# One program for both rounds of local attention and feed-forward, with the next stage's first products among a stage's last steps

## The reference

```python
def _layer(x, wqkv, qs, ksc, wo, lg, lb, w1, b1, w2, b2):
    h = shift_token(x)                      # half the features from the token before
    q, k, v = jnp.split(h @ wqkv, 3, axis=-1)          # 8 heads of 64
    q, k = rotary_xpos(l2norm(q) * qs, l2norm(k) * ksc)
    o = local_attention(q, k, v)            # windows of 64, own and preceding window
    x = x + o @ wo
    h = layernorm(shift_token(x)) * lg + lb
    a, g = jnp.split(h @ w1 + b1, 2, axis=-1)          # 341 features each
    return x + (a * gelu(g)) @ w2 + b2
for l in range(2):
    x = _layer(x, wqkv[l], ...)
```

## Time and profile before

| | |
|---|---|
| three runs | 1767.3, 1768.34, 1778.39 us; median 1768.34 us |
| the profiled execution | span 1763.0 us from its first to its last instruction; the median is 5.3 us more, and no other time of this execution is given |
| busy share of the span | TensorE 90%, VectorE 79%, ScalarE 67%, GpSimd 45% |
| second block | from 778.0 us (first L1319) to 1506.6 us (last instruction ahead of the barrier) |
| its stages begin at | 778.0 (attention), 1063.7 (feed-forward), 1138.8 (attention), 1423.4 (feed-forward) |

### The profile page before, as it was taken

How to read it: one execution, slowest core, us unless ns; L and a number is a source line. 1 busy time by engine, 2 the same in 40 slices (tenths; PEclk the granted TensorE clock), 3 DMA queues, 4 the chain that set the end, 5 groups by cost and what they waited for, 6 DMA issues and landing times. The chain is left out here.

```text
span 1763.0 us, 41286 instructions
## 1 busy us (share of the span) xinstructions
PE 1593.1 (90%) x14986; PEld 813.6 (46%) x14986; DVE 1391.9 (79%) x2949; ACT 1187.9 (67%) x2461; POOL 787.4 (45%) x607
## 2 busy tenths in 40 slices
PE   7499999999999999959999988889999989799887
PEld 4122323322323322236777765557777645444454
DVE  6799999999999999358999976479999869343355
ACT  5178888888888888847787872267878734455521
POOL 4211111221111224338888862188888825544301
PEclk9589999999999999979999999989999999799999
DMA  5203110000000100112232222212232222000001
GB/s 166 70 19 127 43 43 20 20 20 20 21 23 23 30 20 2 49 54 52 61 72 68 57 49 74 54 42 60 55 99 56 56 51 63 1 1 1 1 14 36
DMA packets 124306, 79.02 MB, mean 45 GB/s; under 512 B 50579, under 2 KB 110925, under 8 KB 123853
## 3 DMA queue, kind: packets, MB, share of 16 engines
q1 hardware_dynamic: 122716, 75.31, 16.2%
q10 hardware_dynamic: 1392, 1.12, 0.2%
HBM read 42.82 MB, written 16.79 MB: 34 GB/s over the span
## 5 line engine op out<-in xcount | busy, mean ns | idle before, releaser
L1097 DVE TENSOR_REDUCE hd_top<-hd_pX 128x1 f32<-128x512 f32 x1024 | 623.7, 680 | 33.1 <-PE hd_pX L931 33.1
L1065 ACT ACTIVATE hd_E<-hd_pS 128x1024 f32<-128x1024 f32 x512 | 524.7, 1025 | 82.4 <-PE hd_pS L947 60.4
L931 PE MATMUL hd_pX<-l_K,l_Q 48*128 48x512 bf16 x1024 | 342.5, 396 | 26.1 <-DMA l_Q<-q_parts 21.6
L964 PE MATMUL hd_pO<-hd_E,l_V 128*32 128x256 f32 x4096 | 328.0, 392 | 18.0 <-ACT hd_O L1040 18.0
L947 PE MATMUL hd_pS<-l_Q,l_K 50*128 50x512 bf16 x1024 | 310.8, 384 | 2.8 <-DMA l_Q<-hd_negp 1.8
L879 POOL TENSOR_TENSOR hd_inv<-hd_OS,hd_minus 128x16 f32<-128x16 f32 x31 | 90.0, 2902 | 443.2 <-ACT hd_OS L1053 430.6
L1464 POOL TENSOR_TENSOR w_inv<-w_ss,w_mhalf 128x16 f32<-128x16 f32 x64 | 186.5, 2913 | 0.0
L1429 ACT ACTIVATE w_pS<-w_pS,w_nb 128x128 f32<-128x128 f32 x512 | 178.4, 364 | 7.2 <-DVE w_nb L1513 5.5
L1453 POOL TENSOR_TENSOR w_C<-w_C,w_N 128x1024 f32<-128x1024 f32 x64 | 151.1, 2361 | 65.7 <-DVE w_N L1487 65.5
L964 PEld LDWEIGHTS hd_pO<-hd_E,l_V 128*32 128x32 f32 x4096 | 81.8, 108 | 171.8 <-issue 125.2
L947 PEld LDWEIGHTS hd_pS<-l_Q,l_K 50*128 50x128 bf16 x1024 | 58.9, 94 | 197.9 <-issue 185.0
(11 more groups left out here) (274 smaller groups left out, 2844.4 us busy)
## 6 DMA issues: line engine op xcount, KB each, us to landing
w_VA<-w_V SPq DMA_DIRECT2D x126, 128.0 KB, 2.3
l_Q<-q_parts SPq DMA_DIRECT2D x192, 32.0 KB
l_K<-k_parts SPq DMA_DIRECT2D x168, 32.0 KB
m<-early_rows SPq DMA_DIRECT2D x64, 64.0 KB, 1.7
f_H<-m SPq DMA_DIRECT2D x32, 128.0 KB, 2.8
f_X<-m SPq DMA_DIRECT2D x16, 256.0 KB, 3.1
q_parts<-pj_ptq SPq DMA_DIRECT2D x8, 384.0 KB, 2.5
k_parts<-pj_ptk SPq DMA_DIRECT2D x8, 384.0 KB, 2.5
```

Of the source, the lines that this page charges most:

```text
L931: nc.tensor.matmul(px[:, :], Q[m.j][rows, m.z, b, t * P:(t + 1) * P], K[m.j][rows, b, k * 512:(k + 1) * 512], start=True, stop=True).then_ ...
L964: last = nc.tensor.matmul(pO[VW * b:VW * b + VW, cols], V[n.j][:, b * NT + g, :], E[g % SLOTS][:, b, cols], start=(g == 0 and half == 0), ...
L1065: nc.scalar.activation(E[g % SLOTS][:, 2 * k:2 * k + 2, :], pS[k][:, :, :], ACT.Exp).then_inc(exped[k], 1)
L1097: nc.vector.tensor_reduce(top2[m.z][:, ROW_ORDER[q], k:k + 1], pX[slot][:, :], AX.X, ALU.max).then_inc(topped, 1)
```

## The change

`phase_window_attention` and both uses of `phase_ffn` in the second block become one function, `phase_layers`, with one `nc.Block()` for both layers: 64 tiles and 16 chunks. No barrier stands between its four stages, and their semaphores live until its end, where those of the first block (`heads`) and its own (`layers`) are cleared, one after the other. Before, `heads` was cleared after the first attention.

The feed-forward has no PSUM banks of its own: its three pairs of products use pQK and the two pS, its turned tokens pV (chunk 0: pQK), its down product pO. In chunks 6 and 7 of a layer the three pairs share the two pS, as pQK and pV then serve the next layer's first tiles.

The core of the diff (the operations' bodies change in the names of their banks and in what they count):

```diff
+        def pair(self, k):
+            if self.nn < CHUNKS - 2:
+                return (2, 0, 1)[k]
+            return (k + self.nn) % 2
...
+            def up(n, k):
+                m, p, before = CHUNK[n], CHUNK[n].pair(k), last_use(n, k)
...
+                if before:
+                    pe.wait_ge(hid_ready, KT * before[0] + before[1] + 1)
+                elif p < 2:
+                    for half in range(2):
+                        pe.wait_ge(et_ready[half], tiles - 1 + p)
+                else:
+                    pe.wait_ge(spun, 2 * tiles)
...
-                def lead(n):
-                    if n == TILES - 1:
-                        pe.wait_ge(spun, 2 * TILES)
-                        following.turn(pe, pQK[:, 0, :], ident)
-                steps(pe, step, 3, 2, lead)
+            def attention(layer):
+                first = layer * CHUNKS
...
+                for n in range(0, TILES - 2):
+                    step(layer, n)
+                run(layer, TILES - 2, (turn_c, 0))
+                feed_turn(first)
+                run(layer, TILES - 2, (project, -2), (turn_e, -1, 0), (score, 0), (turn_e, -1, 1), (v, 1), (weigh, -1))
+                run(layer, TILES - 1, (turn_c, 0))
+                up(first, 0)
+                run(layer, TILES - 1, (project, -2), (turn_e, -1, 0), (score, 0), (turn_e, -1, 1))
+                feed_turn(first + 1)
+                run(layer, TILES - 1, (weigh, -1))
+                up(first, 1)
+                run(layer, TILES, (project, -2), (turn_e, -1, 0), (turn_e, -1, 1), (weigh, -1))
+                up(first, 2)
+                run(layer, TILES + 1, (project, -2))
+            def forward(layer):
+                first = layer * CHUNKS
+                for n in range(first + 1, first + CHUNKS - 2):
+                    feed_turn(n + 1)
+                    up(n, 0)
+                    up(n, 1)
+                    down(n - 1)
+                    up(n, 2)
...
+                feed_turn(n + 1)
+                up(n, 0)
+                if following:
+                    turn(next_tile)
+                up(n, 1)
+                down(n - 1)
+                up(n, 2)
+                if following:
+                    qk(next_tile)
+                up(n + 1, 0)
+                if following:
+                    run(layer + 1, -2, (turn, 3))
+                up(n + 1, 1)
+                down(n)
+                if following:
+                    run(layer + 1, -1, (qk, 2))
+                up(n + 1, 2)
+                if following:
+                    run(layer + 1, -1, (turn, 3), (v, 1))
+                down(n + 1)
...
+                gate(first, 0)
+                run(layer, TILES - 1, (take_et, 0, 0), (take_et, 0, 1))
+                gate(first, 1)
+                run(layer, TILES - 1, (take_o, 0))
+                gate(first, 2)
...
+                run(layer, TILES - 2, (bias, 0), (take_v, 1))
+                feed_take(first)
+                run(layer, TILES - 2, (scale_e, 0, 0), (scale_e, 0, 1), (add_x, -1))
+                run(layer, TILES - 1, (bias, 0), (scale_e, 0, 0), (scale_e, 0, 1), (add_x, -1))
+                feed_take(first + 1)
+                hidden(first, 0)
+                feed_stats(first + 2)
+                hidden(first, 1)
+                run(layer, TILES, (add_x, -1))
+                feed.normalise(dve, first + 2)
+                hidden(first, 2)
...
+                    if n == TILES:
+                        chunk_rows(layer * CHUNKS + 2)
+                        feed.load_h(sp, layer * CHUNKS + 2)
...
+                    if n == 2:
+                        chunk_rows(first + CHUNKS - 1)
+                        feed.load_h(sp, first + 3)
...
+                    if n == 5 and layer == 0:
+                        sp.wait_ge(x_stored[0], 16)
+                        for k in range(RING):
+                            load_h(Tile(TILES + k))
```

More of the change, by code:

```diff
@@ L1557, in __init__ @@
         self.var_in, self.rstd_in, self.h_normed, self.turned, self.ht_ready = (
[L1558 removed]
+            s.sem(n) for n in ("var_in", "rstd_in", "h_normed", "turned_f", "ht_ready_f"))
+    CHUNKS = T // CH
     @staticmethod
@@ L1569, in load_h @@
             cols = slice(half * D // 2, (half + 1) * D // 2)
[L1570 removed]
+            sp.dma_start(self.room["H"][:, n % 2, :, cols], self.rows(self.mids[layer][:, 1 - half:1 - half + S, cols], nn))\
                 .then_inc(self.h_in[n % 2], 16)
     def load_x(self, sp, n):
[L1574 to L1581 removed]
+        layer, nn = n // self.CHUNKS, n % self.CHUNKS
+        for r, x in enumerate(self.residuals(layer)):
+            sp.dma_start(self.room[f"X{r}"][:, n % 2], self.rows(x, nn)).then_inc(self.x_in[n % 2], 16)
     def halves(self, pool):
@@ L2395, in build @@
+            room = Scope(nc, rooms, "w")
+            feed = FfnFeed(nc, Scope(nc, rooms, "f"), layers, [pad["m0"], pad["m1"]], tokens["xa"], kept.ffn)
+            into_mixer = MixerStart(nc, mixer, kept)
+            phase_layers(nc, room, layers, kept, start, landed, feed, pad, into_mixer)
+            heads.signals.close()
+            layers.signals.close()
         early.close()
         with ExitStack() as int_room:
-            int_start = IntStart(nc, Scope(nc, int_room, "f2s"), ffn[2], kept, 384)
```

987 lines of the change are left out of this document (621 added, 366 removed).

## The result

The changed kernel takes 1746.8 us in the median (1739.6 to 1754.1, 4 executions), the kernel before 1767.8: a ratio of 0.987, 95% interval 0.983 to 0.992. That is faster by 1.3%, inside the range of 1735 to 1755. The profiled execution of the changed kernel is one of the long ones (1754.1, span 1752.3), that of the kernel before one of the short ones.

A forecast was written before the change was run, and what follows sets the result against it. TensorE was busy 194.84 of 200 us mid-attention, so gains lay only at four stage ends: 5.2 + 15 + 7 - 1.9 = 25.3 off the span of 1763.0, plus 5.3 outside, gave 1743.0 us, range 1735 to 1755.

The forecast's parts named there:

- A: First attention to first feed-forward: chunk 2 turned 7.2 us earlier, less 2.0 for the clock, so 5.2 gained (4.4 to 8.7).
- B: First feed-forward to second attention: first projections moved ahead hide a chain of 14.8 us; 15 gained (12 to 16.4).
- The lower bound of 12: First feed-forward to second attention: the least gain in us, reckoned with each new wait doubled.
- C: Second attention to second feed-forward: earlier copies of turned chunks 2 and 3 gain 7 us (5 to 8.8).
- D: Second feed-forward to mixer, and end: 1.1 us lost to uncovered semaphore clearing, 0.8 to shared bank pairs; -1.9 in all.
- VectorE's arrears: Second feed-forward before the change: copies 12.3 us apart against about 8.7 of TensorE work, as VectorE worked off the first chunks.
- its sign for C: Second feed-forward: second and third copies about 10 to 12 us apart, the first 6.6 earlier.
- The rival's mechanism: Gains partly swallowed: in the second feed-forward an earlier start runs into VectorE's chain, gaining 2 us; total 1753, chance 0.2.
- the 5.3 outside the span: Whole kernel: median 1768.34 us less profiled span 1763.0, added to the forecast span.
- The rival on the clock: Slower: TensorE falls to 1.2 GHz in a feed-forward and stays there, over 1% slower from five chunks on; chance 0.05.

The follow-up runs named there:

- a_undone: Changed kernel with the feed-forward's first products moved back behind the attention's last projection in both layers; second block 708.0 us against 704.6.
- load_late: Changed kernel with chunk 2 loaded only after all rows of the attention have been stored; second block 718.5 us against 704.6.
- all_undone: Changed kernel without inner barriers but with nothing interleaved and chunk 2 loaded late; second block 724.3 us against 704.6, median 1763.7 us.
- b_undone: Changed kernel with the second layer's first projections moved back behind the first feed-forward's last down product; second block 714.5 us against 704.6.
- fill: Changed kernel with three and four unread products on TensorE in the two layers' waits for chunk 2; second block 700.2 us against 704.6.
- sum_late: Changed kernel with GpSimd's residual sum of each layer's chunk 0 moved behind its power for chunk 3; second block 701.6 us against 704.6.
- clear_last: Changed kernel with the first block's semaphores cleared at the very end of the program; second block 703.2 us against 704.6, median 1743.1 us.

## Why the prediction was right, and where it was not

**A** was 5.2, and measured 6.3. The steps held (first products at 1046.35, last `take_et` at 1057.49, load at 1057.59, statistics at 1060.47), the normalisation took 2.05 rather than 2.63, so 8.1 instead of 7.2 at chunk 2, 20.6 behind the last `turn_c` (21.5 forecast). The clock then cost 8.1 - 6.3 = 1.8, for the 2.0 that I took. That the load and the early products both lie on this path was argued from the old rows; a_undone and load_late show it, and all_undone that they pay only together. Of the 8.1, 3.3 is the barrier.

**B** was 15, and measured 22.5 - 6.3 = 16.2. The first tile gained 14.4 (14.2 forecast), the second more, at GpSimd's pace, as forecast; behind the first one the clock is 1.00. The new wait for the token copies is 0.91 (1.2 forecast). b_undone shows that without the interleaving 10.0 of it is lost. The lower bound of 12 doesn't follow from its working: the wait of 1.2 doubled leaves 13.

**C** was 7, and measured 28.7 - 22.5 = 6.2 at chunk 2, 4.6 at the last transposes, or 5.0 without the bank pairs that D counts: mis-sized by 2, at the lower bound. Chunk 2 came later than reckoned, as the normalisation beside two sums took 3.13, not 2.63. Then the clock took another 1.2: the next chunk's transposes follow 11.3 behind those of chunk 2, in the kernel before 10.0. The prediction put that distance down to VectorE's arrears, and its sign for C, copies 10 to 12 apart, failed (13.2). But TensorE was busy for all of the 8 us behind chunk 2's transposes, at 0.63 in the changed kernel, and fill, which leaves VectorE's work as it is, brings the distance to 8.3. The rival's mechanism, VectorE's own chain swallowing an earlier start, shows further on, where fill, sum_late and both end at the same place.

**D** was -1.9, and measured -0.4 for the bank pairs (0.8 forecast) and -1.6 for the longer way to the mixer (1.1 forecast, and clear_last shows 1.1 for the clearing of `heads`): -2.0.

The sum to the mixer was 25.3, and 25.4 was measured; that it is so close is luck, as A and B gave 2.3 more and C 2.0 less. By cause, the 25.4 are 5.7 for the barriers, about 10 for the interleaving in front of the second attention and about 11, the remainder, for the load and the products together, less 1.6 for the mixer.

Two steps outside the sum failed. First, the 5.3 outside the span: it mixed the span of a short execution with the median over short and long ones. In each execution that lists both, the time is 1.7 to 2.1 above the span, 1.8 in that of the changed kernel's profile, so the sum should have given 1737.7 + 1.8 = 1739.5. Second, and the larger: that the time behind the mixer's start stays what it was. In the two profiles of the changed kernel it is 12.0 and 14.7 longer, and five of the ten executions are long, so the median lies between the groups. The rival on the clock was set in the feed-forward, where the clock was back within a chunk of chunk 2's transposes; it was the mixer in which it fell. The forecast of 1743.0 came near the median of 1746.8 by errors of opposite sign, which is luck too.

One reading ahead of the sum was wrong as well: the product of 1.91 behind the barrier is one of two passes (1066.51 in the kernel before), like the one of 1.02, so the low clock nearly doubles its time.

What picks the long rest in an execution stays open. 5 of 10 executions after and 8 of 22 before don't tell whether the change makes it more frequent. The kernel with the six dummies rules out the wait of 8.8 ahead of the mixer, and the low clock behind it, as a necessary cause; nothing tried changed the mixer itself.

## What to carry to other kernels

Where stages are joined, look for the last thing that the next stage waits for, and for what stands ahead of it in the waiting engine's list: here the early load of one chunk and the products that fill the time until it pay only together (load_late loses 13.9, a_undone 3.5, and chunk 2 of the first layer is turned no earlier with either move alone than with neither).

Cut both spans at the ends of the changed part before judging a sum by a median or a small edit by one profile: the part that nobody touched moved by 14.7 behind the block and by 1.6 ahead of it.

A wait of 2.7 or 3.9 us on TensorE cost 1.7 and 2.9 more in the clock behind it. Dummy products in it gave that back, to 0.2; ahead of the mixer, where GpSimd is waited for next, they gave nothing. Real work in the place of the dummies might give the wait back as well; that was not tried.

## What the runs showed of the hardware that I had not expected

The length of a wait alone doesn't decide the clock behind it. A wait of 3.55 was followed by 0.54 and one of 2.72 by products at half speed, but one of 3.63 behind 5.3 us of unbroken dummies was followed by 1.00, and a wait of 2.3 ahead of the last down product by full speed in one kernel and half in another. The same code in two executions shows the same: 16 to 20 us into the block the clock was 0.73 in one and 1.00 in another.

In the mixer the clock can fall to 0.5 to 0.6 while TensorE is busy for 25.23 of 26 us, in code that ran at 1.00 in the profile of the kernel before.
